# Second group of expert tiles: stream 0's combine and the first rope jobs placed five half tiles later, at 2.5 steps per half tile instead of 2.1

## The reference, cut to what matters

```python
x = x + attn_a(layernorm(x))   # 4 encoder layers, 16 heads of 8, alibi + causal mask
x = x + ffn(layernorm(x))      # 8 experts, top 2 of each row, summed with weights
x = x + attn_b(layernorm(x))   # rope attention, causal
x = x + ffn(layernorm(x))      # the same 8 experts again
...
comb = jnp.sum(jax.nn.one_hot(top_i, E) * top_w[..., None], axis=2)
h = gelu(jnp.einsum('bnd,edf->bnef', x, W1) + b1)
y = jnp.einsum('bnef,efd->bned', h, W2) + b2
out = jnp.einsum('bne,bned->bnd', comb, y)
```

## Time and profile before

| | us |
|---|---|
| median of 3 runs | 2834.51 (2833.81 to 2839.74) |
| profiled execution | 2838.04 |
| its span | 2836.3 |
| PE busy in the span | 2449.8 (86%) |
| DVE, ACT, POOL busy | 1864.4 (66%), 1467.7 (52%), 911.5 (32%) |
| granted TensorE clock, mean | 0.948 of full speed |

### The profile page before, as it was taken

The page is one execution under the profiler, slowest core; times in us unless marked ns, Lnnn a source line. Parts: engine busy times, 40 slices in busy tenths (PEclk is TensorE's granted clock), DMA queues, the critical chain, the costliest instruction groups (busy, mean ns, idle before and its releaser), DMA issues.

```text
span 2836.3 us, 52348 instructions
## 1 busy us (share of the span) xinstructions
PE 2449.8 (86%) x19582; PEld 1526.6 (54%) x19582; DVE 1864.4 (66%) x5205; ACT 1467.7 (52%) x2646; POOL 911.5 (32%) x1038
## 2 busy tenths in 40 slices
PE   3799999999999999999999998896878888879964
PEld 2355555554555555545555554586754444547854
DVE  6877777777777777777778885332567777753112
ACT  0356666666666666666665655433234444454421
POOL 6233233333332333333323433231412332322144
PEclk9799999999999999999999999998989899999987
DMA  4252233233323332332312220456721221105754
GB/s 108 74 156 92 96 99 117 79 101 107 95 94 99 95 121 79 99 110 86 98 59 63 80 67 15 132 161 174 212 81 55 67 65 59 59 13 171 211 162 117
DMA packets 158013, 285.56 MB, mean 101 GB/s; under 512 B 22264, under 2 KB 111992, under 8 KB 156024
## 3 DMA queue, kind: packets, MB, share of 16 engines
q1 hardware_dynamic: 149376, 264.23, 30.7%
q0 software_dynamic: 8384, 17.97, 2.1%
HBM read 227.33 MB, written 95.96 MB: 114 GB/s over the span
## 4 chain that ended last, share of the span: by engine, by line
PE 52%; DVE 22%; ACT 12%; issue 5%; POOL 4%; another core or an unknown queue 3%; SPq 1%; DMA 1%; POOLq 0%; ACTq 0%; DVEq 0%
PE bank L589 9%; DVE mx L1215 8%; PE bank L551 7%; PE bank L567 6%; ACT big L816 4%; PE bank L725 4%; PE bank L661 4%; PE bank L735 4%; PE bank L650 4%; PE bank L553 2%; PE bank L517 2%; PE bank L609 2%; POOL big L1509 1%; ACT fhT L847 1%
## 5 line engine op out<-in xcount | busy, mean ns | idle before, releaser
L816 ACT ACTIVATE big<-bank 128x512 f32<-128x512 f32 x1600 | 932.1, 599 | 890.2 <-PE bank L567 496.8
L1215 DVE TENSOR_REDUCE mx<-bank 128x4 f32<-128x512 f32 x1600 | 1049.3, 685 | 421.3 <-PE bank L553 406.4
L551 PE MATMUL bank<-KS,QS 96*128 96x512 bf16 (+3 forms) x2560 | 694.9, 312 | 101.8 <-DVE mx L1215 67.0
L567 PE MATMUL bank<-QS,KS 99*128 99x512 bf16 (+3 forms) x2560 | 629.3, 308 | 34.4 <-ACT big L816 23.7
L1509 POOL TENSOR_SCALAR_AFFINE_SELECT big<-big 128x768 f32<-128x768 f32 (+1 forms) x416 | 265.3, 661 | 770.7 <-ACT big L816 770.7
L553 PE MATMUL bank<-mask_a,ident_b 128*128 128x128 bf16 x2560 | 496.3, 225 | 0.0
L551 PEld LDWEIGHTS bank<-KS,QS 96*128 96x128 bf16 x2560 | 257.4, 101 | 414.4 <-DVE mx L1215 210.6
L589 PE MATMUL bank<-big,V 128*9 128x512 f32 (+3 forms) x5120 | 434.2, 444 | 16.6 <-POOL big L1509 10.8
L567 PEld LDWEIGHTS bank<-QS,KS 99*128 99x128 bf16 x2560 | 215.5, 100 | 165.6 <-ACT big L816 82.6
L884 ACT ACTIVATE big<-bank,big 128x256 f32<-128x256 f32 x368 | 150.8, 471 | 277.7 <-PE bank L725 195.3
L553 PEld LDWEIGHTS bank<-mask_a,ident_b 128*128 128x128 bf16 x2560 | 258.8, 101 | 55.7 <-issue 32.0
(11 more groups left out here) (216 smaller groups left out, 2917.2 us busy)
## 6 DMA issues: line engine op xcount, KB each, us to landing
big<-e_pack SPq DMA_DIRECT2D x92, 578.0 KB
QS<-part_scr SPq DMA_DIRECT2D x480, 96.0 KB
KS<-part_scr SPq DMA_DIRECT2D x480, 96.0 KB
part_scr<-parts SPq DMA_DIRECT2D x80, 384.0 KB
x_rows<-in_alibi SPq DMA_DIRECT2D x47, 384.0 KB, 4.9
y_rows<-in_alibi SPq DMA_DIRECT2D x47, 384.0 KB, 5.5
big<-x_rows SPq DMA_DIRECT2D x92, 128.0 KB
y_rows<-big SPq DMA_DIRECT2D x92, 128.0 KB
```

The lines of the kernel that those rows point to most:

```text
L551: mm(bk[:, col:col + w], Q[0:ROW_MAX, hh, t * P:(t + 1) * P], K[0:ROW_MAX, hh, 0:w], start=True, stop=False)
L567: last = mm(bk[:, col:col + w], K[0:ROWS, hh, t * P:(t + 1) * P], Q[0:ROWS, hh, t * P:T], start=(n == 0 or b + j < CLEARED), stop=(b + j < ...
L816: A(dst, src, ACT.Exp).then_inc(exp_done, 1)
L1215: v.tensor_reduce(dst, src, axis=AX.X, op=ALU.max).then_inc(a_used, 1)
```

## The change

Stream 0 is summed, and job 0's layernorm taken, at q = 12 instead of q = 7 (the POOL power goes with them). The head's first step stands at q = 14 instead of q = 9, and the steps then come at 2.5 per half tile instead of 2.1. By q = 45 either rule has played nearly all of them: 78 of 80 before, 80 now. No instruction is added or left out.

```diff
 SPREAD = (6, 9, 11, 14, 16, 18, 22, 25)
-HEAD_LAG, HEAD_RATE = 8, 2.1
+HEAD_LAG, HEAD_RATE = 13, 2.5
...
         ROUTE = ENC - JOBS
-        COMBINE_FROM, COMBINE_EVERY, COMBINE_BESIDE = (7, 7), (6, 6), (1, 4)
+        COMBINE_FROM, COMBINE_EVERY, COMBINE_BESIDE = (12, 7), (6, 6), (1, 4)
```

## The result

| | before | changed |
|---|---|---|
| median of 13 runs each, us | 2837.45 (2829.60 to 2847.19) | 2846.04 (2840.73 to 2851.96) |
| ratio to before | | 1.0034 [1.0024, 1.0043] |
| profiled execution, us | 2838.04 | 2847.5 |
| its span, us | 2836.3 | 2845.8 |

The account below looks back on a forecast made before the run. The chain of tile store, gathers, sum, layernorm and L450, with PE idle 18.27 us, was taken to set the time at the seam. -5.6 + 1.9 + 1.0 = -2.7 us from 2834.5 gave 2831.8 us, range 2824 to 2840.

Parts of the forecast that it names:

- 0.5 us later, forecast 1.0: Job 0's transposes, L450: gathers beside loads of tiles 31 to 33 delay the start 1.0 us, bounds 0 and 2.3.
- the rival built on it: Gathers ahead of L450 slowed by tile loads: everything behind 6.2 us later, +2.5 us, 2837.0; chance 0.14.
- Pass A was forecast at 2004.7: First chunk of pass A, L551: starts at 2004.7, as before, behind a PE wait of about 9 us.
- The step between projections: Between L450 and pass A: second projection waits for DVE's product, 0.8 us with hand-over, bounds 0 and 1.0.
- The chain from L450: L450 to pass A: 41.2 - 1.7 (one half tile fewer) + 0.8 (projections) = 40.3 us, transfers unchanged.
- PE's wait at L450: Ahead of job 0's transposes: five half tiles played there shrink the wait from 18.3 to about 9 us.
- the 0.8 us that I had given it: Ahead of L450: L735 of tile 26 waits for tile 25's add and slips some 0.8 us.
- The gain of 5.6 us: By pass A's start 26 half tiles are done, not 23: 3 x 1.87 = 5.6 us gained.
- denser head: Pass A's steps with 20 half tiles among them, not 23: PE waits more for DVE, loss 1.0, bounds 0 and 1.5.
- the term for the clock: Behind pass A's start: a 9 us PE wait brings a slow stretch, loss 1.9 us, bounds 0 and 2.0.
- The slower rival: Pass A's steps 30 to 60: one more 8.1 us stall from an unseen source, +7.3 us, 2841.8; chance 0.16.
- The faster rival: Wait ahead of pass A does not grow, as part stores and loads pass sooner: -6.5 us, 2828.0; chance 0.27.

Follow-up runs that it names:

- a: Changed kernel with the head capped at 78 steps until the last half tile, steps 78 and 79 behind the tiles on all engines: 2830.29 us, ratio 1.0012.
- c: Changed kernel at the old density of 2.1 steps per half tile, 12 steps left behind the tiles: 2823.36 us, ratio 1.0001.
- k: The kernel before, unchanged, run again on a third chip: 2829.47 us, ratio 1.0009.
- l: The changed kernel, run again on a third chip: 2841.06 us, ratio 1.0052.
- h: Kernel before with SP alone stopping at 76 steps until the tiles end, other engines' order kept; second chip: 2755.27 us, ratio 0.9998.
- g: Changed kernel with SP alone stopping at 78 steps, other engines' order kept; second chip: 2758.86 us, ratio 1.0023.
- f: Changed kernel with the last two steps behind the last half tile and DVE's maxima for rope jobs 0 and 1 made cheap: 2749.92 us, 0.9981.
- d: Shift of two half tiles instead of five, 2.25 steps per half tile, capped at 78 until the last half tile: 2828.58 us, ratio 1.0007.
- j: Kernel before with a shift of three half tiles, 2.2 steps per half tile, five steps left behind the tiles: 2826.85 us, ratio 0.9998.
- e: Kernel before with DVE's pass A maxima for rope jobs 0 and 1 over 32 of each 128 columns; second chip: 2748.72 us, 0.9978.
- i: Kernel before with, on SP only, step 79's six loads ahead of the last two tile stores; third chip: 2839.42 us, ratio 1.0058.
- b: Kernel before with steps 78 and 79 put ahead of the last half tile on all engines: 2834.38 us, ratio 1.0046.

## Why the prediction was wrong

**Right: L450 and the way to pass A.** POOL's first gather, changed kernel, starts 0.5 us earlier than in the earlier trace rows, and the last issue is 8.86 us behind it, after 8.88:

```profile
1945.03 1.05 POOL L1486 DMA_INDIRECT fp_sb<-y_rows,slots  x1 [28.25 <-DMA y_rows<-big]
...
1953.89 0.94 POOL L1486 DMA_INDIRECT fp_sb<-y_rows,slots  x1 [0.30 <-issue]
```

L450 follows the first gather by 18.35 us, where it was 17.81: 0.5 us later, forecast 1.0. That is only a bound for the gathers, since DVE's sum now starts directly behind an add that had itself been late (1956.62). In a and c DVE does wait for the gathers, and the sum starts 2.4 us behind the end of the last issue where it was 1.6: the gathers beside the tile loads cost 0.9 us there. The rule of the Trainium skill that was set against it (DMA: Bandwidth & Descriptors, "Issuing engines are not separate DMA queues") points the right way, but the rival built on it, 6.2 us, is out. Pass A was forecast at 2004.7 behind some 9 us of waiting, and started at 2005.71 behind 9.21. The step between projections was 0.78 us, forecast 0.8. The chain from L450 took 42.3 us where 40.3 were forecast, and all of the difference lies ahead of the parts' store, which SP issues at 1987.54, 24.2 us behind L450, where the forecast's terms gave 22.3 (1986.57 - 1963.36 = 23.2, less 1.7, plus 0.8). Of these 1.9 us the wait of the V projection L534 for DVE's product, 1.11 us, is the larger part, and I had not counted it. The transfers took 18.2 us from that store to pass A, after 18.0 before. PE's wait at L450 was to be 9 us and is 3.35, mostly because 0.99 + 3.00 us of it moved to the L725 and L735 ahead, the larger one for an add that was late by more than the 0.8 us that I had given it. It changed nothing at L450, and the clock behind it is 0.50 for 4.7 us, as before.

**Wrong by size: from pass A to the last tile.** The gain of 5.6 us was to be cut by 1.9 (clock) and 1.0 (denser head) to a net 2.7, with the stretch itself 5.6 - 1.0 - 1.9 shorter. The stretch grew by 2.7 us instead. The table splits four pairs (the two of the third are from two chips); idle is the stretch less PE's busy time:

| pair | stretch, us | PE busy, us | idle, us | clock |
|---|---|---|---|---|
| before, changed | 80.8, 83.5 | 69.4, 69.2 | 11.4, 14.3 | 0.96, 0.92 |
| k, l (both again) | 86.0, 85.8 | 74.7, 70.6 | 11.3, 15.3 | 0.90, 0.90 |
| before, a | 80.8, 83.1 | 69.4, 68.3 | 11.4, 14.9 | 0.96, 0.91 |
| h, g | 74.3, 73.8 | 70.5, 66.4 | 3.8, 7.4 | 0.94, 0.95 |

The added idleness is 2.9 to 3.9 us in all four, where the term "denser head" had 1.0. The three half tiles less show in the busy time as 0.2 to 4.1 us instead of 5.6, so 1.5 to 5.4 us came back as slower instructions, where the term for the clock had 1.9 (bounds 0 and 2.0). That varies between executions of one kernel: before and k are the same program, with 69.4 and 74.7 us of busy time at 0.96 and 0.90. The slow stretch behind pass A itself was priced right. It is the first of three in the changed kernel; the other two stand behind PE's waits at 2026.34 and 2064.88:

```profile
2005.71:2009.42 3.71, 3.71 (x13) 2.62 (x14) 1.93 (x3) 0.00 (x0) 0.00 (x0) 0.50 0.41 126
2026.48:2029.90 3.42, 3.42 (x13) 2.03 (x12) 1.95 (x4) 1.87 (x6) 0.00 (x0) 0.50 0.45 110
2064.88:2070.86 5.98, 5.98 (x22) 4.38 (x23) 2.66 (x6) 1.91 (x5) 0.00 (x0) 0.50 0.39 130
```

Half of 3.71 us is the 1.9 of the forecast. In all PE works 13.1 us at half clock there, where it was 3.9 before; but in k, the same program as before, it is 14.3, so that growth can't be put down to the change. The term that was surely mis-sized is the denser head, 1.0 us with bounds 0 and 1.5. It was sized where PE was already waiting, at 2071.49; I did not ask how the stretch at 2025 and job 1's projections at 2034 to 2044 would look with less tile work in between. Before, PE's longest wait from 2024 to 2060 was 0.67 us. Now it shows 4.30 us at 2026.34, and at the projections, where it had waited for nothing, 1.10, 1.04 and 0.82 us:

```profile
2034.51 1.12 PE L524 MATMUL bank<-xnT,bp_sb 128*128 128x512 f32 x2 [1.10 <-DVE rtmp L1185]
2039.30 1.12 PE L524 MATMUL bank<-xnT,bp_sb 128*128 128x512 f32 x2 [1.04 <-DVE qk L1183]
2043.92 1.16 PE L534 MATMUL bank<-bp_sb,xnT 128*128 128x128 f32 x8 [0.82 <-DVE rtmp L1185]
```

Those tiles had been cover for more waits than the one that I priced. These three, 2.96 us together, are what the denser head costs wherever it stands at 2.5 steps: they are in a, g and l too, the same to 0.01 us, and in none of before, k and h. With cheap maxima (f) they are 0.70, 0.64 and 0.42 us. The prediction named the projections' hand-over on the way to pass A, but not job 1's. The wait of 4.30 us is another matter: a and l have it (4.81 and 5.21 us), g, on the chip without the long remote stalls, does not. The shift by two, three or five half tiles (d, j, a and c: 0.9998 to 1.0012) is worth nothing that the runs can measure; that DVE's maxima are a part of the reason is indicated by e and f, not shown in the time.

**Missing altogether: SP's queue behind the last tile.** This term, put at nothing without a reason, is what made the kernel slower. The prediction priced no operation there; of the order on SP the text only said that it moves likewise. The number was at hand: HEAD_RATE * (q - HEAD_LAG) is 77.7 at the last half tile with the old constants and 80 with the new, and the profile before shows the exp waiting 6.97 us for y_rows:

```profile
2088.02 1.28 ACT L816 ACT_TABLE_LOAD   x1 [6.97 <-DMA y_rows<-big]
```

The two questions that would have found it are: which of the head's steps end up ahead of the last tile store, and who waits for that store. In the profiled pair the wait is worth 4.7 of the 9.5 us (2.7 to 7.4 us behind the last L735). That SP's order is enough for a loss of the full size is shown by the times of i, and by b with all engines; the traces account for some 5 us of it, and the rest stays open.

**The rivals.** The slower rival came nearest with 2841.8 us, but not by its mechanism. DVE's stalls on a remote source did not double: from L450 to the end of the tiles those of over 3 us sum to 5.21 + 3.15 + 8.11 = 16.5 us before and 5.26 + 6.61 + 5.37 = 17.2 us now. The first and the last of them in the changed kernel:

```profile
1993.91 0.42 DVE L1319 TENSOR_TENSOR big<-bank,big 128x256 f32<-128x256 f32 x1 [5.26 <-remote]
...
2064.13 1.29 DVE L1215 TENSOR_REDUCE mx<-bank 128x4 f32<-128x512 f32 x2 [5.37 <-remote]
```

A further one of 8.32 us, ahead of L450 at 1956.62, is what PE's L735 of 1957.19 waited 3.00 us for, and lies beside the gathers. But one of them, 3.15 us before and 6.61 now, reaches PE where it had not: PE's 4.30 us at 2026.34 stand directly behind it. That much of the rival came true. The faster rival is out, since the wait ahead of pass A grew in full, to 9.21 us. The result lies above the range of 2824 to 2840: 2846.0 by its median, and 2844.1 by the ratio on the 2834.5 us from which the forecast subtracts.

## What to carry to other kernels

When constants shift an order that all engines follow, list for every queue what now stands at the END of the stage, beside what moves at its beginning: a store that somebody waits for must not be issued behind loads that nobody needs yet. Six loads ahead of two stores cost here as much as the whole change lost. And filler that is put into one wait is taken from others: price each wait that it covered, not the one that shows now.

## What the runs showed of the hardware that I had not expected

**Three late DMA engines hold a store.** A pair of tile stores that is issued ahead of the six loads is landed, and its waiter released, 1.8 to 1.9 us after SP's issue ends (before, k); issued behind them, 5.6 to 5.7 us (changed, i), though the DMA engines are far from busy in that time. Their share in the changed kernel (the last but one number), from the stores' issue to their landing:

```profile
2090.00:2092.50 2.50, 1.60 (x15) 1.11 (x13) 1.53 (x3) 0.00 (x0) 0.00 (x0) 1.00 0.63 208
2092.50:2095.00 2.50, 0.00 (x0) 0.00 (x0) 0.00 (x0) 0.00 (x0) 0.00 (x0) 0.95 0.20 79
2095.00:2096.50 1.50, 0.00 (x0) 0.00 (x0) 0.00 (x0) 0.00 (x0) 0.00 (x0) 0.50 0.17 55
```

A share of 0.20 is 3 of 16 engines. The DMA packets in the trace say what these three do (they don't name the engine; three is the number under way). The two stores are 512 packets of 512 bytes, the loads packets of 4096 bytes. Of the stores' packets 416 start between 2091.07 and 2092.37. Then no more than three or four packets are under way at a time, nearly all of them the loads', until 2095.45; and the other 96 packets of the stores, 3/16 of the 512, start at 2095.43. i, l and b show the same: 96 packets follow 3.3 to 3.4 us behind the other 416, as the last load packets go out. In before, k, a and g no store packet is late in this way. So the stores wait for the loads issued ahead of them, on three engines that are behind with these. Before, SP also pauses between the two stores (3.03 us for the pair), but the late packets follow the loads and not that pause. Why three engines are behind no run shows.

**The chips.** They differ more than any edit: the kernel before takes 2837, 2826 and 2826 us on three of them and 2755 us on a fourth, the one called the second above, whose profiled executions show a mean granted clock of 0.960 to 0.963, where the others show 0.947 to 0.952. On the fourth none of DVE's remote stalls of over 3 us appears from L450 to the end of the tiles (e, f, g, h), and PE's idleness from pass A to the last tile is 3.2 to 7.4 us instead of 9.2 to 15.3 (c, whose head goes on behind the tiles, apart). What the source of these stalls is stays open. The Trainium skill (Runtime: NRT & Kernel Launch, "Instruction fetch mechanics") calls the crossing into a new block of instructions mostly hidden; stalls of 5 to 8 us, at the same places of the order in before and k (8.11 us at 2059.28, 8.23 us at 2057.36, each 120 DVE instructions behind the start of stream 0's sum), and none on the fourth chip, neither bear it out nor speak against it, since no row names their source.

Last, the same instructions take different times upstream of the change: the first L450 stands at 1963.36 in one execution of the kernel before and at 1957.31 in another. A difference of a few us between two profiles is therefore worth reading only against a milestone close ahead of it.
